# First tap and bias of two convolutions formed by ScalarE from PSUM instead of by VectorE, with new turn tables

## The reference, cut to what matters

```python
x = x + _L0_attn_ref(_layernorm(x), in_proj_w, conv_w, conv_b, ...)   # state space, 1024 channels
x = x + _L0_ffn_ref(...)                                              # small feed-forward
x = x + _L1_attn_ref(...)                                             # mamba, 256 channels, same convolution
x = x + _L1_ffn_ref(...)                                              # mixture of 8 experts, top 2, GELU
x = x + _L2_attn_ref(...)                                             # linear attention
x = x + _L2_ffn_ref(...)                                              # feed-forward, ternary weights
x = x + _L3_attn_ref(...)                                             # state-space scan
x = x + _L3_ffn_ref(...)                                              # mixture of 8 experts, top 2, gated
...
y = jax.lax.conv_general_dilated(xt, conv_w, window_strides=(1,), padding=[(K - 1, 0)], feature_group_count=D_INNER, ...)
xc = _silu(jnp.swapaxes(y + conv_b[None, :, None], 1, 2))
```

## Time and profile before

| | us |
|---|---|
| median of 3 runs (lowest, highest) | 1424.91 (1422.25, 1425.74) |
| span of the profiled execution | 1400.6 |
| TensorE busy | 1104.8 (79%) |
| TensorE weight loads busy | 698.7 (50%) |
| VectorE busy | 890.9 (64%) |
| ScalarE busy | 630.4 (45%) |
| GpSimd busy | 281.7 (20%) |

### The profile page before, as it was taken

The page is one execution under the profiler, slowest core; times in us unless marked ns, Lnnn a source line. Parts: engine busy times, 40 slices in busy tenths (PEclk is TensorE's granted clock), DMA queues, the critical chain, the costliest instruction groups (busy, mean ns, idle before and its releaser), DMA issues.

```text
span 1400.6 us, 15057 instructions
## 1 busy us (share of the span) xinstructions
PE 1104.8 (79%) x4959; PEld 698.7 (50%) x4959; DVE 890.9 (64%) x1919; ACT 630.4 (45%) x1194; POOL 281.7 (20%) x258
## 2 busy tenths in 40 slices
PE   4978657767977979686768676799999899897791
PEld 2536312334743634353457442574555556787781
DVE  6787879987558767767635789723735652363432
ACT  3433385424552348634237972273252434542330
POOL 3000113324120002130230244202000032014404
PEclk9999877777989999878889897999999999899996
DMA  8100000003520000000125420370000014468782
GB/s 322 47 0 1 0 0 0 0 1 118 163 61 1 0 0 1 0 0 0 45 92 177 131 74 21 96 224 21 1 1 0 1 63 132 157 214 283 260 277 69
DMA packets 49411, 107.02 MB, mean 76 GB/s; under 512 B 4840, under 2 KB 32368, under 8 KB 48688
## 3 DMA queue, kind: packets, MB, share of 16 engines
q1 hardware_dynamic: 44656, 92.74, 20.7%
q0 software_dynamic: 4096, 8.40, 2.0%
q10 hardware_dynamic: 576, 4.87, 0.8%
HBM read 91.24 MB, written 14.75 MB: 76 GB/s over the span
## 4 chain that ended last, share of the span: by engine, by line
PE 41%; DVE 22%; ACT 13%; issue 9%; POOL 7%; DMA 6%; SPq 1%; DVEq 0%; POOLq 0%; ACTq 0%
PE ps L1920 6%; PE ps L1638 5%; DMA expert_ring<-in_e_dram 4%; PE ps L1586 4%; PE ps L1752 4%; DVE up L1341 3%; PE ps L1858 3%; POOL slots_dram L717 3%; ACT big L957 2%; PE ps L1692 2%; PE ps L1829 2%; PE ps L1958 2%; DVE big L1348 2%; POOL up L727 2%; PE ps L1909 1%
## 5 line engine op out<-in xcount | busy, mean ns | idle before, releaser
L1858 PE MATMUL ps<-big,expert_ring 128*128 128x128 f32 x1160 | 158.0, 286 | 33.6 <-DMA expert_ring<-in_e_dram 20.4
L1858 PEld LDWEIGHTS ps<-big,expert_ring 128*128 128x128 f32 x1160 | 145.2, 199 | 48.0 <-DMA expert_ring<-in_e_dram 26.9
L1341 DVE TENSOR_TENSOR_SCAN up<-cv,big 128x512 f32<-128x512 f32 x128 | 152.5, 1230 | 21.5 <-ACT cv L908 17.4
L660 POOL TENSOR_TENSOR rstd<-ve,nhalf 128x4 f32<-128x4 f32 (+1 forms) x41 | 47.2, 1153 | 577.2 <-DVE ve L1119 470.6
L1752 PE MATMUL ps<-big,consts 128*128 128x512 f32 x256 | 154.3, 735 | 2.4 <-DVE big L1348 2.4
L697 POOL TENSOR_TENSOR big<-big,mt 128x512 f32<-128x512 f32 x64 | 85.8, 1344 | 279.1 <-ACT mt L901 152.6
L1920 PE MATMUL ps<-big,weights 128*128 128x512 f32 x256 | 115.4, 597 | 0.0
L1769 PE MATMUL ps<-q,row_pick 96*128 96x512 bf16 x128 | 54.5, 448 | 76.6 <-DVE big L1348 61.4
L1829 PE MATMUL ps<-expert_ring,big 128*128 128x128 f32 x792 | 107.6, 280 | 5.9 <-ACT big L957 3.6
L1829 PEld LDWEIGHTS ps<-expert_ring,big 128*128 128x128 f32 x792 | 98.9, 195 | 15.3 <-ACT big L957 9.8
L1459 DVE SCALAR_TENSOR_TENSOR big<-ps,expert_ring,key 128x128 f32<-128x128 f32 x184 | 51.8, 344 | 79.6 <-PE ps L1858 67.4
(11 more groups left out here) (247 smaller groups left out, 1943.4 us busy)
## 6 DMA issues: line engine op xcount, KB each, us to landing
expert_ring<-in_e_dram SPq DMA_DIRECT2D x46, 836.0 KB, 5.3
expert_ring<-in_e_dram SPq DMA_DIRECT2D x53, 578.0 KB, 4.4
big<-slots_dram SPq DMA_DIRECT2D x21, 256.0 KB, 3.5
results_dram<-mt SPq DMA_DIRECT2D x21, 256.0 KB, 5.3
weights<-in_w_dram ACTq DMA_DIRECT2D x1, 3072.0 KB, 15.5
slots_dram<-big SPq DMA_DIRECT2D x2, 1024.0 KB, 10.3
weights<-in_w_dram SPq DMA_DIRECT2D x1, 1600.0 KB, 8.6
x<-in_x_dram SPq DMA_DIRECT2D x4, 256.0 KB, 13.6
```

The costliest lines, as they stand in the source:

```text
L1341: dve.tensor_tensor_scan(UP[s][:, j, PAD:PAD + T], CV[s][:, j, :], BIG2[s][:, j, :], 0.0, ALU.mult, ALU.add).then_inc(m_scan[s], 1)
L1858: last = pe.matmul(bank4(s, r if m else b % 2)[:, k, :], ring[:, q % RING, r * T + k * P:r * T + (k + 1) * P], XGT[s][:, b // 4 % 4, b % 4 ...
```

## The change

1. ScalarE, after its copy of u to `UP`, issues a second instruction that reads the same PSUM bank and writes tap 3 and bias straight to `CV` (`Identity` with a scale and a bias per channel). In layer 0 it first waits for `l0_xt(b-2)`. `l0_up` (in layer 2 `m_up`) is raised after this second instruction.
2. VectorE's first instruction of each convolution (L1159) is gone, and its wait for `l0_xt(b-2)`. Three instructions are left.
3. Several yields are taken out or moved, so that a step that only waited is folded into its neighbour (TensorE in layers 0, 1, 2 and 5, VectorE in layer 2).
4. All five run-length tables are new, since the steps are counted anew and reordered.

```diff
 RUNS = {
     "pe": [
...
-        1, 1, 1, 2, 1, 6, 1, 22, 75],
+        1, 1, 3, 1, 30, 75],
...
     "sp": [
-        1, 1, 23, 35, 57, 7, 1, 6, 1, 4, 1, 20],
+        1, 1, 23, 35, 56, 1, 1, 2, 1, 8, 1, 16, 1, 10],
 }
...
-                        act.activation(UP[s][:, b % 2, PAD:PAD + T], bank(s, b % 2), ACT.Copy).then_inc(l0_up[s], 1)
+                        act.activation(UP[s][:, b % 2, PAD:PAD + T], bank(s, b % 2), ACT.Copy)
+                        if b >= 2:
+                            act.wait_ge(l0_xt[s], l0_xt.at(s, b - 2))
+                        act.activation(CV[s][:, b % 2, :], bank(s, b % 2), ACT.Identity, bias=pr("conv0_b", b),
+                                       scale=pr("conv0_w", 4 * b + 3)).then_inc(l0_up[s], 1)
...
-                    act.activation(UP[s][:, j, PAD:PAD + T], bank(s, j), ACT.Copy).then_inc(m_up[s], 1)
+                    act.activation(UP[s][:, j, PAD:PAD + T], bank(s, j), ACT.Copy)
+                    act.activation(CV[s][:, j, :], bank(s, j), ACT.Identity, bias=pr("conv1_b", j),
+                                   scale=pr("conv1_w", 4 * j + 3)).then_inc(m_up[s], 1)
...
-            def conv(s, j, wcol, bcol):
+            def conv(s, j, wcol):
 
                 u, v = UP[s], CV[s]
-                step(dve.tensor_scalar(v[:, j, :], u[:, j, PAD:PAD + T], pr(*wcol(3)), pr(*bcol), ALU.mult, ALU.add))
                 step(dve.scalar_tensor_tensor(v[:, j, :], u[:, j, 2:2 + T], pr(*wcol(2)), v[:, j, :], ALU.mult, ALU.add))
...
                     dve.wait_ge(l0_up[s], l0_up.at(s, b))
-                    if b >= 2:
-                        dve.wait_ge(l0_xt[s], l0_xt.at(s, b - 2))
-                    conv(s, b % 2, lambda t: ("conv0_w", 4 * b + t), ("conv0_b", b)).then_inc(l0_cv[s], 1)
+                    conv(s, b % 2, lambda t: ("conv0_w", 4 * b + t)).then_inc(l0_cv[s], 1)
...
                 def turn_block(s, j):
-                    yield
-                    if j >= 2:
-                        pe.wait_ge(l0_yn[s], l0_yn.at(s, j - 2))
                     for c in range(NC):
                         yield
+                        if c == 0 and j >= 2:
+                            pe.wait_ge(l0_yn[s], l0_yn.at(s, j - 2))
```

More of the change, by code:

```diff
@@ L140 @@
     "pe": [
[11 rows of a table removed]
-    "act": [
[8 rows of a table removed]
-    "dve": [
[11 rows of a table removed]
[13 rows of a table added]
+    "act": [
[9 rows of a table added]
+    "dve": [
[11 rows of a table added]
     "pool": [
-        1, 1, 1, 1, 1, 1, 1, 1, 1, 1, 2, 2, 4, 1, 2, 1, 2, 1, 2, 1, 2, 1, 2, 1, 2, 2, 1, 2, 8, 8, 9, 3, 1,
-        9, 1, 4, 1, 1, 1, 1, 1, 17, 1, 2, 14, 3, 1, 3, 1, 4, 1, 4, 1, 2, 1, 1, 9, 1, 10, 3, 1, 1, 18, 19,
+        0, 1, 1, 1, 2, 1, 1, 1, 1, 1, 2, 2, 3, 1, 1, 1, 1, 1, 3, 1, 2, 1, 2, 1, 3, 1, 1, 1, 1, 2, 8, 8, 9, 3,
+        1, 8, 1, 5, 2, 2, 1, 15, 1, 4, 13, 1, 1, 3, 1, 3, 1, 1, 1, 4, 1, 4, 1, 1, 9, 1, 10, 3, 1, 1, 18, 19,
         16, 16],
     "sp": [
-        1, 1, 23, 35, 57, 7, 1, 6, 1, 4, 1, 20],
+        1, 1, 23, 35, 56, 1, 1, 2, 1, 8, 1, 16, 1, 10],
 }
@@ L1312, in mamba @@
                     dve.wait_ge(m_up[s], m_up.at(s, j))
-                    conv(s, j, lambda t: ("conv1_w", 4 * j + t), ("conv1_b", j)).then_inc(m_cv[s], 1)
+                    conv(s, j, lambda t: ("conv1_w", 4 * j + t)).then_inc(m_cv[s], 1)
                 yield
@@ L1333, in mamba @@
                     dve.tensor_tensor(BIG2[s][:, 0, :], bank(s, 2), BIG1[s][:, 2, :], ALU.mult).then_inc(m_scan[s], 1)
-                    yield
-                    dve.wait_ge(m_scan[s], m_scan.at(s, 4 * n))
                     for j in range(2):
                         yield
+                        if j == 0:
+                            dve.wait_ge(m_scan[s], m_scan.at(s, 4 * n))
                         dve.wait_ge(m_da[s], m_da.at(s, 2 * n + j))
@@ L1755, in mamba @@
                 for n in range(NM):
-                    yield
-                    if n == 0:
-                        pe.wait_ge(m_mix[s], m_mix.at(s, 0))
-                        pe.wait_ge(m_sp[s], m_sp.at(s, 1))
                     for k in range(2):
                         yield
+                        if n == 0 and k == 0:
+                            pe.wait_ge(m_mix[s], m_mix.at(s, 0))
+                            pe.wait_ge(m_sp[s], m_sp.at(s, 1))
                         if n and k == 0:
@@ L1904, in ternary @@
                     for r, name in enumerate(("t_w1", "t_w2")):
-                        yield
+                        if j or r:
+                            yield
                         if j >= 2:
@@ L1911, in ternary @@
                 for name, p, src in (("t_h1", t_p1, 0), ("t_h2", t_p2, 4)):
-                    yield
-                    if src == 0:
-                        pe.wait_ge(t_h0[s], t_h0.at(s, 3))
                     for j in range(4):
@@ L1917, in ternary @@
                             yield
+                            if src == j == b == 0:
+                                pe.wait_ge(t_h0[s], t_h0.at(s, 3))
                             if src:
```

## The result

The changed kernel took 1432.58 us (median of 16 runs, 1422.51 to 1442.52) where the kernel before took 1423.06 in the same session (16 runs, 1418.96 to 1433.12): ratio 1.0065, 95% interval 1.0041 to 1.0090. It is slower by 9.5 us by the medians, outside the range of 1400 to 1431. The forecast was 10.8 us faster.

A forecast was written before the change was run, and what follows sets the result against it. No engine was taken to carry the whole time; the chain of waits gave TensorE 41%, VectorE 22%, ScalarE 13%. −2.7 − 2.6 − 5.5 + 0 = −10.8 us from 1424.91 gave 1414.1, range 1400 to 1431.

The forecast's parts named there:

- the 22.8 us: VectorE's 40 instructions of L1159, 570 ns each, taken away by the change; forecast as a fall in busy time, not the gain.
- Part A: Convolutions: first tap moves from VectorE to ScalarE; −5.8 + 1.3 + 1.8 = −2.7 us, ends −5.8 and +4.1.
- two terms for the blocks: Convolution blocks on the chain: 10 led by VectorE each win 0.58 us (−5.8), 12 led by ScalarE each lose 0.11 (+1.3).
- the term for the scans: Four scans on the chain wait for ScalarE's transposes' copy behind a tap: 0.45 us each, 0.69 at most, +1.8 in all.
- The rival in which ScalarE becomes the bound: Layer 0: ScalarE is last in each block, 22 places pay 0.61 us; +7.1 in all, 1432 us, chance 0.13.
- Part B: First mixture of experts: two ScalarE table loads of 1.28 us fewer on the chain, −2.6 us.
- Part C: Last mixture of experts: earlier store, two table loads fewer, changed waits for gathered rows; −2.8 − 1.3 − 1.4 = −5.5 us.
- the last store of stream 0: Last mixture: one read instead of four stands ahead of the store, which leaves at about 1283.3 instead of 1286.05: −2.8 us.
- the sums over the gathered rows: Last mixture, VectorE: one wait of 4.19 us goes, another grows by a 2.8 us step: −1.4, ends −8.7 and +2.8.
- Part D: Folded steps and removed yields: reordering can shift waits; taken as 0, between −5.9 and +5.9 us by the largest such wait.
- The clock rival: TensorE idles ahead of its scans and two run at the lower clock, +17.7 us; +6.9 in all, 1431.8 us, chance 0.07.
- The 24.3 us around it: Median of the kernel before above its profiled execution's span of 1400.6 us; left as it is in the forecast.

## Why the prediction was wrong, point by point

**What bounds the kernel.** Right in that the 22.8 us are no gain. What was read too lightly is the stretch in which VectorE has no idle time: it was left out because the swap takes nothing from it, and yet the reordering could only lose there. From 200 to 300 us, before and after in one session:

```profile
200.00:300.00 100.00, 67.06 (x151) 27.45 (x150) 97.07 (x103) 51.22 (x77) 32.37 (x22) 0.84 0.00 1
```

```profile
200.00:300.00 100.00, 68.62 (x128) 24.82 (x126) 95.48 (x94) 46.51 (x73) 29.06 (x21) 0.76 0.00 0
```

VectorE was nearly as busy (97.1 and 95.5 us) with 103 and 94 instructions; none of the removed first taps lies in this stretch. TensorE had 151 and 128, at 0.84 and 0.76 of its clock. A share of busy time doesn't tell stretched instructions from work.

**Part A (−2.7)** held in its sum: 0.9963 and 0.9992 are −5.2 and −1.1 us. Its two terms for the blocks came out as worked out (0.58 won where VectorE leads, 0.09 for 0.11 lost where ScalarE does), the term for the scans was too small at the first one (1.3 for 0.45). The rival in which ScalarE becomes the bound is out (its time, 1432, was met by chance, since the swap alone loses nothing), and with it what the Trainium skill's page "ScalarE: Activation LUTs", section "Rules for kernel authors", would make of it: the tap is 0.2 us dearer on ScalarE (774 against 570 ns) and still no loss, since it takes 0.58 us a block from VectorE's queue where VectorE leads.

**Part B (−2.6)** failed. The loads were on the chain, but TensorE was next, less than 2.6 us behind, and its own order was new too: the step "the chain runs through it, so it counts in full" left out what is late next. The load itself costs what was said: in the changed kernel a GELU ends at 953.17, the load starts at 953.19.

**Part C (−5.5)** was right in kind, and in size within what the runs can tell (6.5, give or take 4). Its terms were smaller than what came: the last store of stream 0 leaves 0.03 us after its last result, where 2.8 of 5.05 us were to be won, and the sums over the gathered rows no longer wait (0.28 us in all in the second trace of the changed kernel, 8.7 before). VectorE, then SP:

```profile
1299.53 0.29 DVE L1427 TENSOR_TENSOR mt<-ps,expert_ring 128x128 f32<-128x128 f32 x1 [1.05 <-PE ps L1830]
```

```profile
1299.85 0.38 SPq L644 DMA_DIRECT2D results_dram<-mt  x1
```

From 1240 us on TensorE waits 11.6 us for expert weights in the second trace of the changed kernel and 10.2 in the same session's trace of before, so the condition "wrong if TensorE waits for weights by as much more" did not come about.

**Part D (0, ends ±5.9)** is the step that failed. It costs about 19 to 24 us, as what is left over: the changed kernel lost 9.2 us in one session and 12.3 in the other (1.0065 and 1.0088), and the swap (3 and 5.2) and the last mixture (6.5) won something that the rest of the order had to eat first. All terms but this one were worked out from an order that was looked at; for this one a single wait bounded a table that moves hundreds of steps. A wait of this size for each stretch in which two streams are interleaved, of which there are at least three here, would have given about ±18 us, and even that only just reaches what was lost.

**The clock rival** had the right sign and almost the right time (1431 for 1432.6), but at 0.07 it was not the forecast, and its cause is only in part borne out. Its test was a rise of TensorE's busy time by more than 5 us. The two first traces, of different sessions, have 1104.8 and 1104.2. In one session it is 1098.8 before, 1094.8 with the swap alone, 1089.8 with the order alone and 1110.8 in the changed kernel, so the test says yes for the changed kernel and no for the order alone, which is slower than before all the same. Over all runs of that session the mean granted clock is 0.893, 0.894, 0.894 and 0.890. By the 5.3 us for 0.01 that is about 2 of the 17 us between the swap alone and the changed kernel, an estimate, and which of the two is the cause no run separates. Within the 16 runs of the changed kernel the clock goes with the time too: 1422.5 us at 0.888, 1442.5 at 0.876.

**The span.** The 24.3 us around it were most likely a session's difference. It did no harm to the sum, but it was a warning that the trace and the times came from different conditions.

## What to carry to other kernels

When a change comes with a new instruction order, the order is a change of its own: price it by stretches, first those where an engine has no idle time, and keep its range as wide as one such wait for each stretch. Split the two on the chip as soon as possible; here the last mixture's order alone gained, the swap alone cost nothing, and the rest of the order ate both. Before the order of one queue is mended, look at what the next queue holds: here a wait of 5.61 us on VectorE became one of 3.65 us behind ScalarE, and nothing was won. And take two traces of each kernel before a lateness of a few us is explained.

## What the runs showed of the hardware

VectorE's scans of 1.20 us took up to 2.67 us beside a GpSimd product in SBUF (second trace of the changed kernel). With the product in pieces of 8 columns the longest took 1.67 us in the old order and 1.41 in the new, and the means were 1217 and 1216 ns. And in some sessions TensorE, VectorE and ScalarE pause while GpSimd issues 16 indirect transfers, where in others they don't, with the same kernel; one chip had a session of either kind. ScalarE's longest single wait there is 13 to 17 us in the 11 traces that have the pause. ScalarE in the slower trace of the swap-only kernel, from 1240 to 1340 us (waited for, us in all, times, longest):

```profile
ACT key L960 <- remote: 33.0, 3, 15.1
```

What holds them is not in the trace.
